# Row copies from SP's and ScalarE's queues for five groups of the linear passes of a GNN stack

## What is computed

```python
edge_index = jnp.stack([src, dst])
h = jnp.maximum(_layernorm(x, axis=-1), 0.0)
x = x + _L0_gnn_ref(h, edge_index, ...)             # attention, one head
h = jnp.maximum(_layernorm(x, axis=-1), 0.0)
x = x + _L1_gnn_ref(h, ..., src, dst, edge_type_8)  # relational
h = jnp.maximum(_layernorm(x, axis=-1), 0.0)
x = x + _L2_gnn_ref(h, edge_index, ...)             # two GCN convolutions
h = jnp.maximum(_layernorm(x, axis=-1), 0.0)
x = x + _L3_gnn_ref(h, edge_weight, ..., edge_index) # attention, four heads, twice
```

```python
proj = jnp.einsum('ni,rio->nro', h, W)      # L1: 8 relations, W from 4 bases
msg = proj[src, rel_type]
agg = jax.ops.segment_sum(msg, dst, num_segments=h.shape[0])
out = h @ root_weight + agg + bias
...
norm = dinv[src] * dinv[dst]                # L2, for each of its two convolutions
msg = h[src] * norm[:, None]
out = jax.ops.segment_sum(msg, dst, num_segments=n_nodes)
```

## Time and profile before

| | us |
|---|---|
| median of 3 runs | 4416.87 (4411.13 to 4417.32) |
| the profiled execution | 4409.67 |
| its span, first to last instruction | 4407.6 |
| GpSimd busy | 2373.4 (54%) |
| TensorE busy | 2787.0 (63%) |
| VectorE busy | 2064.7 (47%) |
| ScalarE busy | 1555.5 (35%) |
| LIN[0], first gather to last addition | 963 to 1556 |
| LIN[1] | 1610 to 2151 |
| LIN[2] | 2180 to 2717 |

### The profile page before, as it was taken

How to read it: one execution, slowest core, us unless ns; L and a number is a source line. 1 busy time by engine, 2 the same in 40 slices (tenths; PEclk the granted TensorE clock), 3 DMA queues, 4 the chain that set the end, 5 groups by cost and what they waited for, 6 DMA issues and landing times.

```text
span 4407.6 us, 52138 instructions
## 1 busy us (share of the span) xinstructions
PE 2787.0 (63%) x15364; PEld 2038.6 (46%) x15364; DVE 2064.7 (47%) x4219; ACT 1555.5 (35%) x3919; POOL 2373.4 (54%) x2449
## 2 busy tenths in 40 slices
PE   3177887972323357877768877466666764666667
PEld 2055665632222244554445554255555543555555
DVE  5033343642222245665545555245555653555557
ACT  2044444530000043333433333144444523444443
POOL 2745555126666636666466663535555544555553
PEclk9976666875555568899789897578887886778778
DMA  4322222131111122221222221444544435444441
GB/s 86 68 58 61 61 60 60 19 135 46 47 47 46 46 61 51 54 53 51 64 50 53 53 53 32 124 130 134 139 135 133 123 87 135 133 130 138 134 136 49
DMA packets 351654, 360.72 MB, mean 82 GB/s; under 512 B 125198, under 2 KB 274389, under 8 KB 351381
## 3 DMA queue, kind: packets, MB, share of 16 engines
q0 software_dynamic: 89600, 211.77, 18.3%
q1 hardware_dynamic: 255638, 143.69, 12.6%
q10 hardware_dynamic: 6148, 1.93, 0.3%
HBM read 327.08 MB, written 30.26 MB: 81 GB/s over the span
## 4 chain that ended last, share of the span: by engine, by line
PE 35%; another core or an unknown queue 18%; issue 17%; DVE 15%; POOL 9%; ACT 3%; SPq 1%; DMA 1%; DVEq 1%; ACTq 1%; POOLq 0%
PE QX L1364 19%; POOL gathered_rows L549 9%; PE NU L1364 9%; PE MTB L1364 5%; DVE sums_transposed L834 3%; DVE extra_sums_transposed L834 2%; DVE query_key_products L834 2%; DVE gathered_rows L834 1%; DVE messages L834 1%; PE MID L1364 1%; DVE scan_scores L981 1%; ACT window_distance L698 1%; SPq L436 1%; ACTq L601 0%
## 5 line engine op out<-in xcount | busy, mean ns | idle before, releaser
L532 POOL DMA_INDIRECT gathered_rows<-key_value_rows,src_index x832 | 831.0, 999 | 684.3 <-DVE messages L834 389.3
L834 DVE TENSOR_TENSOR sums_transposed<-sums_transposed,NU 128x512 f32 x624 | 425.7, 682 | 1089.5 <-remote 777.1
L549 POOL DMA_INDIRECT gathered_rows<-gcn_rows,src_index x720 | 684.3, 950 | 465.6 <-issue 196.8
L532 POOL DMA_INDIRECT gathered_rows<-gat_rows,src_index x416 | 397.1, 955 | 384.5 <-DVE messages L1007 182.3
L1364 PE MATMUL NU<-start_penalty,zero_weights 128*128 128x512 bf16 x624 | 279.5, 448 | 420.4 <-DVE sums_transposed L834 323.3
L549 POOL DMA_INDIRECT gathered_rows<-relation_rows,src_relation_index x416 | 401.2, 964 | 208.1 <-issue 120.1
L794 ACT ACTIVATE gathered_rows<-iota_window,dst_in_window_by_edge 128x128 f32<-128x128 f32 x832 | 265.1, 389 | 605.6 <-remote 375.3
L729 ACT ACTIVATE edge_node_onehot<-iota_window,dst_in_window_by_edge 128x128 f32<-128x128 f32 x1248 | 394.9, 387 | 159.7 <-remote 146.5
L1364 PEld LDWEIGHTS NU<-edge_node_onehot,messages 128*128 128x128 f32 x2496 | 419.4, 236 | 68.3 <-issue 47.8
L1364 PE MATMUL NU<-edge_node_onehot,messages 128*128 128x128 f32 x2496 | 421.6, 321 | 42.5 <-issue 42.1
L1364 PE MATMUL NU<-gathered_rows 128*128 128x128 f32 x2496 | 397.4, 311 | 65.8 <-issue 28.9
(11 more groups left out here) (294 smaller groups left out, 4299.6 us busy)
## 6 DMA issues: line engine op xcount, KB each, us to landing
query_window<-query_rows SPq DMA_DIRECT2D x832, 66.0 KB
dst_in_window_row<-dst_in_window SPq DMA_DIRECT2D x156, 256.0 KB
gathered_rows<-key_value_rows,src_index POOLq DMA_INDIRECT x832
relation_rows<-gathered_rows SPq DMA_DIRECT2D x25, 512.0 KB
gathered_rows<-gcn_rows,src_index POOLq DMA_INDIRECT x720
dst_in_window_row<-src_place_and_block SPq DMA_DIRECT2D x28, 256.0 KB
gathered_rows<-gat_rows,src_index POOLq DMA_INDIRECT x416
query_window<-gat_target_scores SPq DMA_DIRECT2D x416, 2.0 KB
```

The lines of the kernel that those rows point to most:

```text
L532: pool.indirect_dma_start(out=rows_of(a, s)[:, t, :], out_offset=None, in_=a["table"], in_offset=bass.IndirectOffsetOnAxis(ap=srcI[:, TPG ...
L549: pool.indirect_dma_start(out=linear_rows(p["k"], k)[:, t, :], out_offset=None, in_=p["table"], in_offset=bass.IndirectOffsetOnAxis(ap=p[" ...
L834: return dve.tensor_tensor(o, x, y, op)
```

## The change

Five groups are no longer fetched by GpSimd's gathers. In LIN[0] these are group 56 and group 103, copied by SP, and group 80, copied by ScalarE; in LIN[1] and LIN[2] group 100, copied by SP. A new function copy_rows goes over the 128 edges of a tile position (lanes): for each it loads four byte offsets (row_at) into registers and issues four DMAs of one row, 512 B. Four small VectorE instructions (row_offsets) make the offsets from the indices once. In LIN[0] SP does both of its groups in one go after the tables and the sources' places are stored; in the GCN passes it does LANES = 10 lanes behind each load of places. The rows have buffers of their own (own_rows, three slots), so GpSimd's ring passes over these groups. TensorE waits for two semaphores in such a group, one for each pair of tiles. Some unused semaphores are dropped.

```diff
@@ -65,6 +65,8 @@
     LRING = 8
     TURN, LEAD = 7, 5
     AHEAD = 4
+    BY_SP, BY_ACT = [(56, 103), (100,), (100,)], [(80,), (), ()]
+    LANES = 10
     HEADS, HD = 4, D // 4
     NREL, NBASE = A["L1_gnn_w_comp"].shape
     BIG = 1e30
@@ -187,6 +189,7 @@
         done_mark = sb("done_mark", [1, 1])
         sbrow = sb("tile_backward_row", [1, P])
         wcomp = sb("relation_coefficients", [P, NREL * NBASE])
+        row_at = sb("row_byte_offsets", [P, 4, TPG], i32)
 
 
...
+        own_rows = [flat_win[:, q * SPAN:(q + 1) * SPAN].rearrange("p (t d) -> p t d", d=D) for q in (2, 3)]
+        own_rows.append(STa[:].rearrange("p a n -> p (a n)").bitcast(f32).rearrange("p (t d) -> p t d", d=D))
+        OWN = {(0, 56): (0, 0), (0, 103): (1, 1), (0, 80): (2, 2), (1, 100): (2, 3), (2, 100): (2, 3)}
...
+        rows_in = [[sem(f"row_copies_in_{i}_{h}") for h in range(2)] for i in range(4)]
...
-        FETCHED = [(p, k) for p in range(3) for k in range(NG) if not by_matmul(p, k)]
+        FETCHED = [(p, k) for p in range(3) for k in range(NG) if not by_matmul(p, k) and (p, k) not in OWN]
...
         def linear_rows(p, k):
             if by_matmul(p, k):
                 return picked
+            if (p, k) in OWN:
+                return own_rows[OWN[p, k][0]]
             q = FETCH_NO[p, k] % LRING
             return lrows[:, TPG * q:TPG * q + TPG, :]
 
@@ -357,6 +366,18 @@
             held = [engine.alloc_register(f"{name}_{t}") for t in range(n)]
             engine.load(held, at)
             return [engine.snap(r, donate=True, min_val=0, max_val=top) for r in held]
+
+
+        def copy_rows(engine, name, p, k, lanes):
+
+            slot, i = OWN[p["k"], k]
+            table = p["table"].rearrange("n d -> (n d)").bitcast(u8)
+            top = 4 * D * ((NV if p["k"] else NV * NREL) - 1)
+            for e in lanes:
+                at = load_values(engine, row_at[e:e + 1, i, :], f"{name}_row_{p['k']}_{k}_{e}", TPG, top)
+                for t in range(TPG):
+                    engine.dma_start(own_rows[slot][e:e + 1, t, :].bitcast(u8),
+                                     table[ds(at[t], 4 * D)].unsqueeze(0)).then_inc(rows_in[i][t // 2], 16)
 
 
         @block.sync
@@ -463,6 +484,11 @@
                     sp.dma_start(drow_sb[:, done % 2, :].rearrange("p (a e) -> p a e", a=2),
                                  srow_d[:, k * SPAN:(k + 1) * SPAN].unsqueeze(0).broadcast_to([P, 2, SPAN])
                                  ).then_inc(S[f"place_in{done % 2}"], 16)
+                    if q == 0:
+                        sp.wait_ge(S["row_at_ready"], 2)
+                        if p == 2:
+                            sp.wait_ge(S["rows_used"], NG + BY_SP[1][0] + 1)
+                    copy_rows(sp, "sp", LIN[p], BY_SP[p][0], range(min(P, LANES * q), min(P, LANES * q + LANES)))
 
             store_tables(1, [(rel_d.rearrange("(n r) d -> n (r d)", r=NREL), NREL * D, 0)])
             sp.wait_ge(S["src_split_ready"], 1)
@@ -471,8 +497,12 @@
                              src_split[:, w, 0:3 * P].rearrange("p (j e) -> p j e", e=P)).then_inc(S["src_rows_stored"], 16)
                 sp.dma_start(srow_d[w, 3 * P * P:EP].rearrange("(t e) -> t e", e=P),
                              src_split[0:T - 3 * P, w, 3 * P:4 * P]).then_inc(S["src_rows_stored"], 16)
+            tables_stored(1)
+            sp.wait_ge(S["src_rows_stored"], 16 * 4)
+            sp.wait_ge(S["row_at_ready"], 1)
+            for k in BY_SP[0]:
+                copy_rows(sp, "sp", LIN[0], k, range(P))
             store_tables(2, [(gcn_d, D, 0)])
-            sp.wait_ge(S["src_rows_stored"], 16 * 4)
             picked_inputs(1, 2)
             store_tables(3, [(gcn_d, D, 0)])
             picked_inputs(2, 3)
@@ -539,7 +569,7 @@
                 for slot in range(NSLOT):
                     pool.wait_ge(S[f"tstored{slot}"], TOTAL[n][slot])
                 for k in range(NG):
-                    if by_matmul(p["k"], k):
+                    if by_matmul(p["k"], k) or (p["k"], k) in OWN:
                         continue
                     q = FETCH_NO[p["k"], k]
                     if q >= LRING:
@@ -755,6 +785,11 @@
                 act.wait_ge(S["deg_psum"], j + 1)
                 act.activation(dinvT[:, j * 256:(j + 1) * 256], QXf[j % 2][:, 0:256], ACT.Sqrt, bias=1.0
                                ).then_inc(S["deg_sqrt"], 1)
+            for slot in range(NSLOT):
+                act.wait_ge(S[f"tstored{slot}"], TOTAL[1][slot])
+            act.wait_ge(S["row_at_ready"], 1)
+            for k in BY_ACT[0]:
+                copy_rows(act, "act", LIN[0], k, range(P))
             norm_tables(2, 2)
 
             def graph_norm(j):
@@ -1277,6 +1312,15 @@
             then(dve.reciprocal(exN2[:, 0:NBK, 3], exN2[:, 0:NBK, 2]))
             dve.wait_ge(S["deg_sqrt"], 1)
             then(dve.reciprocal(dinvN[:, 0:NBK], dinvN[:, 0:NBK]))
+            def row_offsets(p, idx):
+
+                for (q, k), (_, i) in OWN.items():
+                    if q == p:
+                        last = dve.tensor_scalar(row_at[:, i, :], idx[:, TPG * k:TPG * k + TPG], 4.0 * D, None, ALU.mult)
+                last.then_inc(S["row_at_ready"], 1)
+
+            row_offsets(0, relI)
+            row_offsets(1, srcI)
             norm_tables(0, 1, 1)
             linear(LIN[0])
             dve.memset(done_mark[:], 0.0).then_inc(S["numT_ready"], 1)
@@ -1564,10 +1608,12 @@
                     pe.wait_ge(S["s_ready"], SBASE[3 + p["k"]] + k + 1)
                     if by_matmul(p["k"], k):
                         pe.wait_ge(S["picked_rows"], TPG * (PICK_NO[p["k"], k] + 1))
-                    else:
+                    elif (p["k"], k) not in OWN:
                         q = FETCH_NO[p["k"], k]
                         pe.wait_ge(lgathered[q % LRING], 16 * TPG * (q // LRING + 1))
                     for t in range(TPG):
+                        if (p["k"], k) in OWN and t % 2 == 0:
+                            pe.wait_ge(rows_in[OWN[p["k"], k][1]][t // 2], 16 * 2 * P * max(1, p["k"]))
                         last = mm(NU[k % 2][:, ds(off[t], P)], linear_rows(p["k"], k)[:, t, :], Sl[:, k % GPC, t, :],
                                   False, t == TPG - 1)
                     last.then_inc(S["rows_used"], 1)
```

12 lines of the change are left out of this document (6 added, 6 removed).

## The result

| | before | after |
|---|---|---|
| median of 4 runs, us | 4415.34 (4411.13 to 4417.32) | 4677.84 (4673.62 to 4701.29) |
| ratio | | 1.0608 (95%: 1.0577 to 1.0639) |
| LIN[0], from the mark ahead of its tables to its last | 677.5 | 932.2 |
| LIN[1] | 595.4 | 603.8 |
| LIN[2] | 566.3 | 572.6 |

The rows of the passes are from one profiled execution each. The changed kernel is 6.1% slower, 262 us, and 254.7 us of it are LIN[0]. Faster was forecast, 4405 us. The untouched ATT[2] differs by 9.7 us between the two profiled executions, so the 8.4 and 6.3 us of the GCN passes can't be read from these two alone.

A forecast was written before the change was run, and what follows sets the result against it. GpSimd's gathers were taken to bound the first linear pass, TensorE the two GCN passes. Terms: -14.9 gathers, +0.7 VectorE, +2 end of pass, 0 GCN passes, sum -12.2, giving 4405 us; range 4394 to 4436.

The forecast's parts named there:

- SP's pace: First linear pass, SP's row copies: 0.45 us per copy, 2.15 per lane, group 103 done at 1530, just hidden.
- bounds for a copy: Price of one row copy, from rows of other shapes: 0.21 to 0.71 us, SP's end between 1310 and 1875.
- SP is late: Rival, first linear pass: copy pitch above 0.45 makes group 103 the end; at 0.50, 4449 us; chance 0.17.
- GpSimd's held time: First linear pass: 66.3 us in 21 waits, taken as not directly touched by the change.
- GpSimd's 14.9 us: First linear pass: 12 gathers fewer at 1.245 us each, 14.9 us saved, all on the path.
- late end: Rival, end of first linear pass: SP ends near 1545 or a burst gives back 5 to 12 us; 4408 to 4416; chance 0.21.
- GCN passes: Group 100's four gathers removed in each pass: gain 0, bounds a gain of 5.0 or a loss of 10 each.
- Late rows: First linear pass: rows land late in bursts, so GpSimd is held by the ring of eight groups, 66.3 us.
- contention: Rival, first linear pass: 1536 row copies delay the gathers' landing, each of 21 waits grows 1.5 us; 4434; chance 0.07.

## Why the prediction was wrong

**SP's pace: the step that failed.** The prediction took 2.15 us for a lane, from window copies at 2876 us, and an end of SP at 1530. Measured: 825.3 us for 256 lanes, 3.22 each, and 1811. The row was sound for what it showed (the fast condition has 0.49 per copy, 1.97 per lane, under the 2.15), but it lies in a stretch in which GpSimd issues no gathers (the last is at 2864.71, the row at 2876.23), and LIN[0] has gathers from end to end. Eight copies in 22.40 us were in the same trace. The 5.04 us of the earlier trace rows, which the prediction put down to semaphores, were a sign too: GpSimd had gone on gathering at 498.36, and the time over the usual is one copy of the eight, of 1.46 us. The prediction's bounds for a copy, 0.21 and 0.71, came from instructions of other shapes, and shape was not what mattered; even so their far end of 1875 held the true 1811, and neither the range nor the chances made use of it.

**The rival.** "SP is late" had the right place and the right mechanism, with its point at a pitch of 0.47. Its price, 4449, was for a pitch of 0.50. The mean pitch was 825.3 / 1024 = 0.81. With that pace the rival's own working gives 985 + 825 = 1810, which is what happened; the range ended at 4436.

**A second step: that GpSimd's held time is independent of the change.** TensorE reached group 56 well before SP had it. GpSimd was held 113.6 us, and SP got its best pace just then. In the slow condition the two therefore pay each other: without that hold SP would have ended later still.

**ScalarE.** Forecast 2.3 us per lane and an end at 1275; measured 3.5 and 1422.5, stretched like SP's. In the fast condition 2.2 and 1036. It is hidden in both, as forecast.

**GpSimd's 14.9 us.** Shown in the fast condition: the last gather ended at 1255.7 in place of 1266.1, in a pass that began 2.4 us later, so 12.8 earlier. There 10.3 of it went into the wait for group 103, which was the "late end" rival with SP as its cause, and LIN[0] gained 0.9.

**GCN passes.** Forecast 0. In the fast condition they gained 4.4 and 5.2, close to the 5.0 that the prediction held for a bound; in the slow one nothing is shown.

**Late rows and contention.** The prediction read GpSimd's waits and VectorE's 19.74 us as rows that land late in bursts. The packets of the gathers say otherwise (2.2 us by the median in either condition). Contention of transfers falls too: waits of GpSimd for unnamed completions were 66.3 us and then 65.2, and the DMA share stayed at 0.18 beside gathers. The Trainium skill ("DMA: Bandwidth & Descriptors", Issuing engines are not separate DMA queues) says that issuing from several engines saves only the time on the sequencer that starts a transfer. That time was the whole matter here: 1024 copies cost SP's queue 504 us in the fast condition and 825 in the slow one.

**The condition.** In the fast condition the median fell by 7.2 us, near the forecast 12.2, but by luck: by the traces LIN[0], which was to give all of it, gave 0.9, and the GCN passes, which were to give nothing, gave 9.6. The profile of before was taken in the slow condition, and its signs were there, in waits and in SP's moves; a move of line 436 never lasts over 38 ns in the fast one:

```profile
DVE sums_transposed L834 <- remote: 777.1, 134, 23.2
...
L436 SPq MOVE query_window<-query_rows x832: 2/29/1399, 2831.9 to 4316.5; - x167
```

The prediction saw such waits and took them as late rows rather than as queues that stand still.

## What to carry to other kernels

A price for an instruction of a queue is only as good as the company of the row it is read from: find rows of the same queue while the engine that will run beside it is running, and look at the longest instruction of a cheap kind (a register move) before trusting a median. A run of a thousand small instructions with an average need of 0.5 us has no slack against a neighbour that costs it 0.7 on average; put the last group that the pass needs on a queue that is done long before, and give a queue one such group, not two (shown in the fast condition alone). And where a trace has long waits whose releaser it can't name, first ask which engine is at work in all of them.

## What the runs showed of the chip that I had not expected

- The same kernel takes 4407 to 4415 us in some sets of runs and 3576 to 3582 in others, 23% apart, and each is steady within its set. The runs don't tell what sets it. The verdict of the change turns on it: 1.0608 in one, 0.9972 to 0.9981 in the other.
- In the slow condition a run of gathers (0.944 us each, one in 1.25) slows SP's queue by a mean of 0.77 us per gather in LIN[0] and of 1.0 in ATT[0] (22.40 - 3.94 us in 18 gathers), ScalarE's by (348.97 - 340 x 0.55) / 244 = 0.66; moves, register loads and DMA issues alike. The slowing builds up over a run of gathers (0.64 us per copy at its start, 2.66 or more after 42 us) and lasts on after it (eight copies in 14.80 us behind the last gather). In the fast condition a gather is as long, and SP keeps its 0.49 us per copy. Which part of a gather does it was not tried.
- A copy of one row of 512 B, with its address from a register, costs the issuing queue 0.23 us into SBUF and 0.54 into DRAM, and a register load of four offsets 0.56.
